# Order of the matmuls inside an attention score: the plain fp32 product behind the three split products

## What is computed

```
xn = layernorm(x)
s  = attention(xn; wq, wk, wv, wo)      # 32 query heads, 8 key/value heads of 128, rope,
                                        # token i sees j with i-128 < j <= i, out @ wo
g  = silu(ffn(xn; w1, w3, w2))          # weights are 4-bit values times a scale per 64
x  = x + s * g
```

## Time and profile before

| | us |
|---|---|
| median of 3 runs | 802.6 |
| the profiled execution | 802.51 |
| its span, first to last instruction | 800.7 |
| TensorE matmuls (PE), busy | 796.0 |
| TensorE weight loads (PEld), busy | 671.8 |
| VectorE (DVE), busy | 567.6 |
| GpSimd (POOL), busy | 475.4 |
| ScalarE (ACT), busy | 428.9 |

### The profile page before, as it was taken

One profiled execution on the slowest core, in us unless ns is written; L12 is line 12 of the kernel. 1 busy time (PEld: TensorE's weight loads), 2 busy tenths in 40 slices (PEclk: granted clock), 3 DMA queues, 4 the chain that ended last, 5 costly groups with the idle time before them and its releaser, 6 DMA issues.

```text
span 800.7 us, 13470 instructions
## 1 busy us (share of the span) xinstructions
PE 796.0 (99%) x3966; PEld 671.8 (84%) x3966; DVE 567.6 (71%) x1636; ACT 428.9 (54%) x1104; POOL 475.4 (59%) x357
## 2 busy tenths in 40 slices
PE   9999999999999999999999999999999999999998
PEld 7888888888888888888888888888888888888887
DVE  7725867667448867777786777778677777867785
ACT  5413313223138675666666565666656566665672
POOL 2103314224256774867487486748757674878997
PEclk9999999999999999999999999999999999999999
DMA  9659425201000400400040040004004000420102
GB/s 273 192 180 271 135 71 158 78 28 53 2 27 14 132 14 1 132 2 14 2 131 13 0 131 0 13 0 131 13 0 130 1 13 0 131 65 0 40 1 106
DMA packets 51909, 54.00 MB, mean 67 GB/s; under 512 B 4129, under 2 KB 33185, under 8 KB 51873
## 3 DMA queue, kind: packets, MB, share of 16 engines
q1 hardware_dynamic: 51728, 53.50, 22.2%
q10 hardware_dynamic: 144, 0.07, 0.0%
HBM read 47.25 MB, written 6.29 MB: 67 GB/s over the span
## 4 chain that ended last, share of the span: by engine, by line
PE 92%; POOL 4%; issue 2%; DMA 1%; ACT 0%; SPq 0%; DVE 0%; POOLq 0%; ACTq 0%
PE bank L1332 26%; PE bank L1333 26%; PE bank L1334 26%; PE bank L1523 3%; PE bank L1539 3%; PE bank L1556 2%; PE bank L1557 2%; PE bank L1558 2%; PE bank L1565 1%; POOL swap L453 1%; PE bank L1562 1%; PE bank L1563 1%; DMA raw<-in_wv 1%; POOL acc L484 1%; POOL q L457 1%
## 5 line engine op out<-in xcount | busy, mean ns | idle before, releaser
L453 POOL TENSOR_TENSOR swap<-swap,cst 128x512 f32<-128x512 f32 x80 | 108.1, 1351 | 41.7 <-ACT swap L697 41.7
L718 ACT ACTIVATE probs<-probs,nmx 128x128 f32<-128x128 f32 x256 | 100.0, 392 | 59.7 <-DVE nmx L1106 59.7
L1332 PE MATMUL bank<-xh,wih 128*128 128x512 f32 x320 | 128.9, 403 | 0.0
L1333 PE MATMUL bank<-xl,wih 128*128 128x512 f32 x320 | 125.2, 391 | 0.0
L1334 PE MATMUL bank<-xh,wil 128*128 128x512 f32 x320 | 125.0, 391 | 0.0
L1332 PE MATMUL bank<-woh,oh 128*128 128x512 f32 (+1 forms) x260 | 100.8, 388 | 0.0
L1333 PE MATMUL bank<-wol,oh 128*128 128x512 f32 (+1 forms) x260 | 100.6, 387 | 0.0
L1334 PE MATMUL bank<-woh,ol 128*128 128x512 f32 (+1 forms) x260 | 100.5, 387 | 0.0
L401 POOL TENSOR_TENSOR hl<-act_h,hh 128x512 fp32r<-128x512 f32 x22 | 31.6, 1436 | 99.5 <-ACT hh L599 99.5
L457 POOL TENSOR_TENSOR q<-q,swap 128x512 f32<-128x512 f32 x64 | 86.0, 1344 | 6.6 <-DVE q L1081 1.6
L476 POOL TENSOR_TENSOR ph<-ph,cst 128x512 fp32r<-128x512 f32 x32 | 41.9, 1309 | 73.2 <-ACT ph L733 73.2
(11 more groups left out here) (139 smaller groups left out, 2025.8 us busy)
## 6 DMA issues: line engine op xcount, KB each, us to landing
raw<-in_wq SPq DMA_DIRECT2D x32, 256.0 KB, 4.7
raw<-in_wo SPq DMA_DIRECT2D x32, 256.0 KB, 4.8
pk<-in_w SPq DMA_DIRECT2D x44, 128.0 KB, 3.6
sc<-in_s SPq DMA_DIRECT2D x44, 128.0 KB, 3.7
vals<-stage SPq DMA_DIRECT2D x16, 256.0 KB, 2.9
vraw<-vals SPq DMA_DIRECT2D x16, 256.0 KB, 2.9
pk<-in_w SPq DMA_DIRECT2D x11, 256.0 KB, 2.6
sc<-in_s SPq DMA_DIRECT2D x11, 256.0 KB, 3.0
```

What stands on the lines that cost most here:

```text
L453: nc.gpsimd.tensor_tensor(v, v, spread(sin.unsqueeze(1), P, 2, SEQ), ALU.mult).then_inc(sin_done, 1)
L718: e = nc.scalar.activation(probs[:, s, c0:c1], probs[:, s, c0:c1], ACT.Exp, bias=nmx[:, s, i:i + 1], scale=-1.0, accum_out=rsum[:, s, i:i ...
L1332: nc.tensor.matmul(out_, sh, mh, start=(i == 0), stop=False)
L1333: nc.tensor.matmul(out_, sh, ml, start=False, stop=False)
```

## The change

Within `scores` the plain product goes from the first place to the last. The wait for `klq_done` stays directly ahead of the split products, so for b = 0 it now stands ahead of everything in the score. The increment of `scores_ps` goes to the plain product, which is now last. No instruction is added or taken away.

```diff
                     pe.wait_ge(rope_done, cnt(5, g, bp, h + 2))
                 wait(pe, masked, cnt(8, g, bp, s - 1))
                 c = b * SEQ
-                nc.tensor.matmul(S_B[s % 2][:, 0:P], q[:, h, c:c + P], k[:, bp, c:c + P], start=True, stop=True)
                 if b == 0:
                     pe.wait_ge(klq_done, cnt(5, g, bp, h + 2))
                 three(S_B[s % 2][:, P:3 * P], [(qh[:, h, b, :], ql[:, h, b, :], kh[:, bp, c:c + SEQ],
-                                                kl[:, bp, c:c + SEQ])]).then_inc(scores_ps, 1)
+                                                kl[:, bp, c:c + SEQ])])
+                nc.tensor.matmul(S_B[s % 2][:, 0:P], q[:, h, c:c + P], k[:, bp, c:c + P], start=True, stop=True) \
+                    .then_inc(scores_ps, 1)
```

## The result

The changed kernel takes 804.65 us (median of 11 runs, 804.4 to 805.39), the kernel before 802.66 (11 runs, 802.43 to 803.49). The ratio is 1.0024, with a 95% interval of 1.0016 to 1.0032. The prediction was 802.4 us with a range up to 804.0 and no difference as the likeliest case: wrong, by 0.65 us beyond the range and in the sign.

What follows compares the result with a forecast made beforehand. TensorE's matmuls, 99% of the span, were taken as the bound. Terms of -0.4 (entry), 0 (exit) and +0.2 (wait) gave -0.2 us against 802.51, so 802.3, and 802.4 as the median; range 801.3 to 804.0.

Steps and rivals of the forecast that it cites:

- The bound: TensorE's matmuls cover 99% of the span, so the sum of distances between matmul ends sets the end.
- own sign of an error: In the changed profile TensorE should be busy within 1 us of 796.0.
- The wait for `klq_done`: At b = 0, 64 times, ql must be ready 0.22 us sooner: bounds 0 and 0.34 us, 0.2 taken.
- Rival A: Late ql stalls TensorE at head 3 of b = 0 in every step: 4.0 us slower, 806.4; chance 0.07.
- Weight loads: q's load now lies beside a 256-wide pass instead of a 512-wide one, at 79 places: costed at nothing.
- rival B: q's load isn't covered by a split pass, at 79 places: 5.5 us slower, 807.9; chance 0.02.
- The exit: Plain product ahead of the 512-wide passes, 79 times: -0.5 to +1.1 us in all, 0 taken.
- Neighbours: At 49 junctions where one score follows another, the cycle is only entered at another point: costed at nothing.
- entry: A split pass now follows the 512-wide pass, 79 times: -0.8 to 0 us in all, -0.4 taken.
- Rival C: Transitions at the 79 places are worth more than the rows show: 2.1 us faster, 800.4; chance 0.08.

Runs made afterwards that it cites:

- wait_first: Against the kernel before, only the wait for `klq_done` moved, to ahead of the plain product, which stays first in all scores: 802.72 us, ratio 0.9999.
- pairs_only: Against the kernel before, wait first everywhere and the plain product last only in scores that stand together (48 places): 804.16 us, ratio 1.0019.
- exit_split: Against the kernel before, wait first; pairs go split, plain, plain, split; single scores keep the plain product first: 802.57 us, ratio 0.9997.

## Why the prediction was wrong

**The bound** was right: TensorE's passes set the end, and the chain of waits is the view in which the loss is found. The prediction's own sign of an error came true: TensorE is busy for 2.4 us more, where it allowed 1.

**The wait for `klq_done`** was priced well. For the first step it had 0.09 us and the trace shows 0.10; for the last 0.25, and 0.27 is there; the usual steps show none. That little of it reaches the end was right too: the wait alone costs nothing that the run can tell (`wait_first`). Rival A did not happen.

**Weight loads, rival B:** the plain product behind a split pass takes 0.22 us, as said. No load sticks out.

**The exit** is the step that failed most. The prediction measured the nearest rows, transposes, over six passes, found ends of -0.006 and +0.014 us per place, and took 0. (The mean of its five rows is 1.378, not 1.376, which moves both ends by 0.002, or 0.2 us in all, and changes nothing else.) The six passes behind a pair do take 1.39 us now (432.06 to 433.45), inside those ends. But the disturbance goes on to the tenth pass, past the window that I had chosen because it was long enough for the rows of before. Over ten passes it is +0.026 for pairs, and it is +0.024 for the scores ahead of `attend`: 49 x 0.026 + 15 x 0.024 = 1.6 us, where the term had 0 and its upper end +1.1. The transposes don't show it: behind eight of them the disturbance is 16 ns.

**Neighbours and entry** were treated as settled, the first at nothing, the second as a gain of 0.4 us. Scores in a pair take 8 ns more, single ones 1 to 2: 49 x 0.008 + 30 x 0.0015 = 0.4 us of loss. The argument that the cycle "is only entered at another point" counts each transition once and takes it to be independent of what stood before it. It isn't: a split pass behind the plain product takes 121 ns in the new order and 119 in the old. And 0.01 us rows can't carry a term that is worth 0.005 at 79 places.

Together 1.6 + 0.4 = 2.0 us, against 1.99 between the medians. That it meets so closely is in part luck: the medians carry some tenths of noise. Rival C was right that transitions are worth more than the rows show, and had the wrong sign.

**What stays open** is why. The disturbed passes behind pairs are 3 to 10 ns long beyond their 227, in a pattern that repeats in every steady step. It is the same ahead of `project` and of `out_project`, so there neither the operands nor the waits of the next matmul make it. Behind the single score ahead of `out_project` the pattern of the same order changes from step to step (19 to 38 ns before, 10 to 44 in `pairs_only`), so something besides the order has a part, and no run here varied it. DVE stands idle at the first disturbed pass behind the pair at 432.06 (its next instruction starts at 432.26 after 2.58 us of idle time), so its access is not needed for that one; for the later passes, and for the other engines, nothing was ruled out. Whether the weight loads and the matmuls drift in their timing against each other was not settled by any run; the loads of q being 191 ns on average in the new order, against 188, would fit it and shows no more than that.

## What to carry to other kernels

Where one engine is busy for 99% of the span, the order of its instructions has a price of its own even if every wait, load and count stays the same: here 34 ns at each pair and 26 at each score ahead of `attend`, 0.24% in all. To price a new order, take the distance between two marks a whole step apart, or sum over all passes until they are regular again, and don't count a transition by itself; rows of 0.01 us don't resolve it. If a short matmul of another kind must stand among wide ones, try it first or in the middle of the narrow ones: behind pairs and ahead of `attend` every order tried that was left by it disturbed the passes behind more. Ahead of `out_project` the difference was small (36 ns against 31 on average). The best order here (`exit_split`) is not measurably faster than the kernel before.

## What the runs showed of the hardware that I had not expected

- Behind short passes the wide ones are longer for up to ten passes, some 2.3 us. How far it reaches depends on the order of all the narrow passes and not only on the last: behind pairs that end with the plain product 35, 46 or 53 ns in sum over ten passes. It does not depend on that order alone: the same order at the same place gave 10 to 44 ns in one run (`pairs_only`, ahead of `out_project`).
- The records of q's weight loads are longer in the new order. In the changed kernel (min/median/max, ns), against 186/188/189 in the earlier trace rows:

```profile
L1527 PEld LDWEIGHTS bank<-k,q x256: 187/192/193, 247.9 to 779.6; 128*128 128x128 f32 x128
```

- Two fp32r passes of 128 columns take 0.06 + 0.11 us where the two fp32 ones take 0.22, and the next pass gives all of it back (0.17 us for 0.12).
